# Attention with 32x32 block transposes on VectorE and P x V in 32-row, 64-column TensorE tiles

## What is computed

```python
q = rmsnorm(x @ wq_a.T) @ wq_b.T            # 32 heads, 64 plain + 64 rotary columns
kv = rmsnorm(ckv) @ wkv_b.T                 # ckv: 64 latent columns for all heads
scores = einsum("bqhd,bkhd->bhqk", q_full, k_full) * scale
scores = where(causal, scores, min)
attn = softmax(scores, axis=-1)
out = einsum("bhqk,bkhd->bqhd", attn, v)    # B=2, S=1024, H=32
out = out.reshape(B, S, H * VD) @ wo.T
```

## Time and profile before

| | |
|---|---|
| median of three runs | 2180.91 us (2177.37 to 2185.91) |
| the profiled execution: its own time | 2179.61 us |
| the profiled execution: span of the trace | 2177.8 us |
| TensorE matmuls busy, share of the span | 94% |
| VectorE, ScalarE, GpSimd busy | 52%, 44%, 52% |

### The profile page before, as it was taken

One profiled execution on the slowest core, in us unless ns is written; L12 is line 12 of the kernel. 1 busy time (PEld: TensorE's weight loads), 2 busy tenths in 40 slices (PEclk: granted clock), 3 DMA queues, 4 the chain that ended last, 5 costly groups with the idle time before them and its releaser, 6 DMA issues. The chain is left out here.

```text
span 2177.8 us, 36515 instructions
## 1 busy us (share of the span) xinstructions
PE 2045.7 (94%) x11088; PEld 1617.7 (74%) x11088; DVE 1131.3 (52%) x2607; ACT 965.1 (44%) x2162; POOL 1122.5 (52%) x834
## 2 busy tenths in 40 slices
PE   1899798999999999999999999999969999996999
PEld 1688688777777777777777777777748888875787
DVE  6655276566656666666666566666642111114453
ACT  3221075566666666666666666666641101003110
POOL 2331110888888888888888888888600000004321
PEclk9999999999999999999999999999989999998999
DMA  5652242111121122112111211221174232304421
GB/s 147 210 174 105 86 131 90 46 41 56 59 64 36 53 65 65 39 54 65 39 55 59 64 36 53 65 65 34 38 230 130 81 112 82 110 35 177 145 88 67
DMA packets 96888, 182.59 MB, mean 84 GB/s; under 512 B 16576, under 2 KB 53568, under 8 KB 94528
## 3 DMA queue, kind: packets, MB, share of 16 engines
q1 hardware_dynamic: 96832, 181.87, 26.5%
HBM read 122.85 MB, written 58.98 MB: 83 GB/s over the span
## 5 line engine op out<-in xcount | busy, mean ns | idle before, releaser
L951 PE MATMUL psS<-keyT,q 128*128 128x256 f32 (+2 forms) x2304 | 514.0, 358 | 4.3 <-POOL q L1168 4.3
L951 PEld LDWEIGHTS psS<-keyT,q 128*128 128x128 f32 x2304 | 382.9, 189 | 87.0 <-DVE negmax L1098 26.3
L1037 ACT ACTIVATE prob<-prob,negmax 128x128 f32<-128x128 f32 (+7 forms) x512 | 393.2, 771 | 74.7 <-DVE negmax L1098 74.7
L1098 DVE CUSTOM_DVE_ANT_0 prob<-psS,mask 128x128 f32<-128x128 f32 (+7 forms) x512 | 381.7, 755 | 80.4 <-PE psS L951 55.3
L1044 ACT ACTIVATE pT<-psT 128x512 f32<-128x512 f32 (+2 forms) x384 | 202.1, 526 | 350.1 <-PE psT L962 348.4
L1129 DVE COPY pT<-psT 128x256 f32<-128x256 f32 (+3 forms) x384 | 196.9, 513 | 305.1 <-PE psT L962 302.2
L962 PE MATMUL psT<-ident,prob 128*128 128x128 f32 x2304 | 338.1, 274 | 1.7 <-ACT prob L1037 1.1
L482 PE MATMUL f_psy<-f_weff,f_xT 128*128 128x512 f32 x1344 | 311.4, 391 | 0.0
L1326 PE MATMUL o_psy<-o_w,o_o 128*128 128x512 f32 x1344 | 304.8, 389 | 0.0
L962 PEld LDWEIGHTS psT<-ident,prob 128*128 128x128 f32 x2304 | 268.6, 140 | 33.0 <-issue 11.4
L1326 PEld LDWEIGHTS o_psy<-o_w,o_o 128*128 128x128 f32 x1344 | 252.3, 188 | 52.4
(11 more groups left out here) (108 smaller groups left out, 2017.5 us busy)
## 6 DMA issues: line engine op xcount, KB each, us to landing
wo<-in_wo SPq DMA_DIRECT2D x16, 1024.0 KB, 5.3
o_scale<-row_scales SPq DMA_DIRECT2D x64, 256.0 KB, 3.4
oT<-o_sum SPq DMA_DIRECT2D x128, 128.0 KB, 2.3
o_in<-oT SPq DMA_DIRECT2D x32, 512.0 KB, 5.2
f_xt<-in_x SPq DMA_DIRECT2D x16, 512.0 KB, 4.1
f_w_in<-in_w SPq DMA_DIRECT2D x16, 512.0 KB, 6.3
w_sum<-f_w_in SPq DMA_DIRECT2D x16, 512.0 KB, 5.1
x<-f_xo SPq DMA_DIRECT2D x16, 512.0 KB, 2.6
```

The lines of the kernel that those rows point to most:

```text
L951: ins = nc.tensor.matmul(psS[:, li % 2, shift + x0:shift + x1], q[:, s % 2, a, t * P:(t + 1) * P], k.keyT[:, m, b * S + x0:b * S + x1], st ...
L1037: nc.scalar.activation(row, row, ACT.Exp, bias=negmax[:, li % 8:li % 8 + 1], scale=-1.0, accum_out=rowsum[:, col:col + 1]).then_inc(exped, 1)
L1098: nc.vector.tensor_tensor_reduce(out=prob[:, li % 4, 0:(t + 1) * P], in0=place(s, t), in1=k.mask[:, S - (t + 1) * P:S], scale=-1.0, scalar ...
```

## The change

A step is now a pair of heads in one batch: 32 steps of 16 tiles (`n`; tile `t = n // 2`, head `e = n % 2`). T moves from TensorE to VectorE, which turns each 32x32 block in place. So row group `i` (partitions 32i to 32i+31) of `pT` holds 32 keys of a block and the queries of the i-th quarter of a tile. P x V therefore runs in eight tiles of 32 rows and 64 columns: four row groups, each with a PSUM bank of its own, and two halves of the output for the two heads. The values are loaded once, after the latents phase has stored them, with each 32-key block in each of the four row groups (`val`, 32 DMAs).

```diff
-    for kt in range(blocks):                                   # T on TensorE
-        ins = nc.tensor.transpose(psT[...], prob[:, (QT * s + t) % 4, ...], k.ident[:])
+    nc.vector.transpose(pT[t // 4][:, n % 2, t % 4, 0:width],  # T on VectorE
+                        prob[:, n % RING, 0:width]).then_inc(turned, 1)
```

```diff
-    for half, kts in enumerate(columns):                       # V
-        ins = nc.tensor.matmul(psV[half * KVR:(half + 1) * KVR, n0:CHUNK], k.val[:, b * QT + kt, :],
-                               pT[ch][:, kt, n0:CHUNK], ...)
+    for kt in kts:
+        t0 = max(kt - 4 * ch, 0)
+        for a in range(BLOCKS):
+            for e in range(2):
+                for i in range(BLOCKS):
+                    rows, x = slice(32 * i, 32 * i + 32), kt * P + 32 * a
+                    ins = nc.tensor.matmul(psV[KVR * e:KVR * e + KVR, i, 32 * t0:P].rearrange(...),
+                                           val[rows, b, a, kt, :], pT[ch][rows, e, t0:QT // 2, x:x + 32], ...)
```

```diff
-    nc.scalar.activation(qf[:, ch, :], psM[:, :], ACT.Copy)    # Q: one copy, and four GpSimd operations
+    nc.scalar.activation(qf[:, n % 2, :], psV[:, n, :], ACT.Copy)
+    nc.scalar.activation(swapped[64:96, n % 2, :], psV[96:128, n, :], ACT.Copy)
+    nc.scalar.activation(swapped[96:128, n % 2, :], psV[64:96, n, :], ACT.Copy)   # and three on GpSimd (A)
-    nc.vector.tensor_copy(q[..., HI, ...], qf[...])            # high part of q
+    nc.scalar.activation(q[..., HI, ...], qf[...], ACT.Copy)   # H; the low part (B) stays on GpSimd
```

```diff
-    # join on VectorE, then scale on GpSimd
+    for i in range(BLOCKS):                                    # O on VectorE: scale out of PSUM
+        ins = nc.vector.tensor_tensor(by_block(o_sum[:, ch, :], i), psV[:, i, 0:P].rearrange(...),
+                                      by_block(o_scale[:, ch, :], i), ALU.mult)
```

```diff
+PARTS = ((0, (0, 1, 2, 3)), (1, (0, 1)), (1, (2, 3)), (1, (4, 5, 6, 7)))       # V0: queries 0-511; V1 to V3: 512-1023
+PE_STEP = ("F1+0 Q0+1 S12+0 S13+0 Q1+1 S14+0 W0+0 S15+0 Q2+1 Q3+1 S0+1 S1+1 S2+1 S3+1 S4+1 S5+1 S6+1 S7+1 V1+0 V2+0 "
+           "V3+0 S8+1 S9+1 V0+1 S10+1 F0+1 S11+1")
+POOL_STEP = ("A1-1 B0-1 B1-1 A2-1 A3-1 B2-1 B3-1 A0+0")
```

More of the change, by code:

```diff
@@ L939, in scores, with queries @@
-            def scores(it, s, t):
-                li, b = QT * s + t, (s // 2) % 2
-                if later(it * TILES + li - 1, 1):
-                    pe.wait_ge(maxed, it * TILES + li - 1)
+                ins.then_inc(f_done, 1)
+            def queries(it, n, s):
+                ch, e, b = n // 2, n % 2, s % 2
+                pe.wait_ge(f_split, folds(it, e, s - s % 2 - 1))
+                for i, (a, m) in enumerate(PASSES):
+                    for t in range(QRT):
+                        ins = nc.tensor.matmul(psV[:, n, :], wq[:, a, e, t, :], k.qnT[:, m, t, b * S + ch * CHUNK:b * S + (ch + 1) * CHUNK],
+                                               start=(i == 0 and t == 0), stop=(i == 2 and t == QRT - 1))
+                ins.then_inc(q_done, 1)
@@ new lines, in query_hi, with exponentials @@
+            def query_hi(it, n, s):
+                act.wait_ge(roped, (it * 2 + s) * 4 + n + 1)
+                nc.scalar.activation(q[:, n % 2, HI, n // 2 * CHUNK:(n // 2 + 1) * CHUNK], qf[:, n % 2, :], ACT.Copy).then_inc(q_hi, 1)
+            def exponentials(it, n, s):
+                step, width = it * 2 + s, (n // 2 + 1) * P
+                act.wait_ge(maxed, step * TILES + n + 1)
+                if n % 8 == 0 and later(step, 2):
+                    act.wait_ge(recip, step * 2 - 3 + n // 8)
+                row = prob[:, n % RING, 0:width]
+                nc.scalar.activation(row, row, ACT.Exp, bias=negmax[:, n % 8:n % 8 + 1], scale=-1.0,
+                                     accum_out=rowsum[:, column(n, s):column(n, s) + 1]).then_inc(exped, 1)
@@ L1125, in copy_turned @@
[L1125 to L1130 removed]
+                    dve.wait_ge(valued, (step - 1) * NV + (1 if t < 4 else NV))
+                nc.vector.transpose(pT[t // 4][:, n % 2, t % 4, 0:width], prob[:, n % RING, 0:width]).then_inc(turned, 1)
@@ L1180, in body @@
+            pool.wait_ge(tab_in, 48)
             def body(r):
-                jobs = list(r.jobs(POOL_STEP))
-                job, n, s = list(STEADY.jobs(POOL_STEP))[-1]
-                before = None if r.first else (job, n, s - 4)
-                for job, n, s in jobs:
+                job, n, s = list(Round(0).jobs(POOL_STEP))[-1]
+                before = None if r.first else (job, n, s - 2)
+                for job, n, s in r.jobs(POOL_STEP):
                     if before:
-                        pool.wait_ge(q_lo if before[0] == "Q" else o_scaled, r.it * 8 + 2 * before[2] + before[1] + 1)
+                        pool.wait_ge(roped if before[0] == "A" else q_lo, (r.it * 2 + before[2]) * 4 + before[1] + 1)
```

506 lines of the change are left out of this document (235 added, 271 removed).

## The result

The changed kernel takes 2589.1 us (median of 4, 2577.0 to 2605.9) against 2181.9 us before: a ratio of 1.187 (95% interval 1.180 to 1.194). It is slower by 407 us. The forecast was 2100 us and the range ended at 2265 us, so both the sign and the range were missed.

What follows compares the result with a forecast made beforehand. TensorE's list was taken to set the pace at 37.4 us a step; the path's terms summed to 34.5, gaining 93 us over 32 steps and losing 14 at the ends: 2179.6 - 93 + 14 = 2100 us, range 2020 to 2265.

Steps and rivals of the forecast that it cites:

- (1): TensorE's P x V jobs V1 to V3: 5.9 us, plus 0.5 for drain and handover, 6.4 us a step.
- (2): VectorE's O operations for queries 512 to 1023, four that overlap a little: 0.9 us.
- (3): SyncE's O store, then scales stored, read back and landed, while VectorE waits for `o_scale`: 7.3 us.
- (4): Second O 0.9, the query matmuls in its bank 1.7, three copies 1.8: 4.4 us.
- (5): GpSimd's eight operations on the queries, with ScalarE's high parts fitting between: 11.0 us.
- (6): Zigzag of scores and maxima from tile 1 to tile 7, with a VectorE transpose and R: 4.5 us.
- V0's 2.4 us: TensorE's first P x V job, four blocks of each width: 2.4 us, ending 3.5 us before the scales land.
- second rival: VectorE's transposes cost twice the copies' slope, 9.1 us more: step about 38.0 us, 2212 us; chance 0.10.
- The clock: TensorE's granted clock was read as 1.00 (2.4 GHz) in the attention phase of the kernel before.
- The first rival: Row tiles in P x V don't pass one another: V1 to V3 11.8 us, step 40.4 us, 2290 us; chance 0.15.
- its break-even of 16 ns a pass: Step breaks even at 37.0 us, V1 to V3 at 8.4 us: 16 ns pass to pass, against 11.5 counted.
- The third rival: Almost no gain: each wait a little longer, or TensorE's 768 loads a step at 14 to 17 ns: 2150 to 2200 us; 0.10.

Runs made afterwards that it cites:

- v_looped: Changed kernel with P x V issued from short inner loops repeating key tiles, 832 passes a step, TensorE's loop body 1511 instructions instead of 3541: 2269 us.
- v_quarter: Changed kernel with P x V done only for the first 32 keys of every 128, three quarters of that product left out: 2210 us.
- pe_unrolled: Changed kernel with TensorE's list written out for all 16 pairs in place of a loop, nothing left out: 2502 us.
- v_looped_wide: As v_looped, but each P x V pass moves both heads' columns and every second key block is left out, so about half the passes: 2229 us.
- v_half: Changed kernel with P x V done only for the first 64 keys of every 128, TensorE's loop body 2005 instructions: 2296 us.

## Why the prediction was wrong, point by point

The terms of the prediction's path, beside one step of the changed kernel (1001.65 to 1052.86, the rows above) and one of v_looped (1004.48 to 1044.66), in us:

| term | forecast | changed kernel | v_looped |
|---|---|---|---|
| (1) V1 to V3 with handover | 6.4 | 15.0 | 9.0 |
| (2) first O | 0.9 | 0.9 | 0.9 |
| (3) until the second O begins | 7.3 | 8.4 (behind V0) | 6.8 (behind `o_scale`) |
| (4) second O, Q, copies | 4.4 | 9.8 | 7.1 |
| (5) GpSimd's eight operations | 11.0 | 11.0 | 10.9 |
| (6) zigzag to V1 | 4.5 | 6.1 | 5.5 |
| sum | 34.5 | 51.2 | 40.2 |

- **The step that failed** is "If all eight tiles run side by side, it takes two pass lengths ... 5.9 us", term (1), and with it V0's 2.4 us. It counted what the array does, and put at nothing what it takes to bring 1536 instructions a step to it. Measured: 14.8 us from V1's start, and 5.8 us for V0. Pages fetched too slowly are by far the larger part. The array's part was nearly right: at the full clock a quarter of V1 to V3 took 1.91 us (v_quarter), and less the 0.22 us of its last pass, four such quarters are 6.8 us (an estimate). The miss of 0.9 us there is mostly in the narrow passes, put at 0.11 us for 16, 6.9 ns each; pe_unrolled's last piece of V3 has them at 10.4 ns ((1.26 - 0.22) / 100). The other 8 us of the 14.8 are stalls for pages, and the lower clock behind them.
- Of the 15.7 us between the forecast's step and the measured one, the loop adds 3.6 us (50.2 to 46.6), the rest of the fetching some 7.1 us (46.6 to 39.5), and 0.8 us (39.5 to 38.7) go with fewer passes and hidden turns. By the medians these three are 2.7, 7.3 and 1.2 us a step; the changed kernel's profiled execution was the slowest of its four. As v_looped has more passes and its inner loops' turns, the share of the fetching is probably put too low.
- What is left, 38.7 against 34.5 us, are mostly terms (4) and (6). The first queries' matmuls stand on TensorE behind scores, and in every second step behind the folds too. In v_looped, from 600 to 1400 us, (4) averages 7.1 us in the steps with folds and 4.7 in the others, where I counted 4.4 (the step shown has folds; the next, without, took 38.0 us). I read the path in the right order, but in (4) left out the folds, which stand ahead of Q in the list. The fetching and the order of SyncE were undone by runs, one at a time; (4) and (6) are read from timelines and not tested.
- **The clock.** The forecast took 1.00 throughout. The stretch shows 0.85, with the passes behind stalls at the lower level (2.92 us for six against 1.56). It came back to 0.99 when the stalls went (v_looped), so it is a consequence of TensorE's idle time and not its cause; but not of the fetching alone, since it stayed at 0.85 in v_quarter, where TensorE waited for other engines. How many of the 7.1 us are its share, no run separates.
- **VectorE** was right: 1.241 us for 1024 columns (1.25 forecast), O at 0.284, and it is never the bound. The second rival falls: 1024 columns take 1.24 us, not 2.3. GpSimd, the lengths of SyncE's operations and the order of the path were right.
- **The first rival** had the sign and not the mechanism: row tiles do pass one another (v_looped_wide). Straight code stays below its break-even of 16 ns a pass: 14.3 ns at 128 columns and less at fewer.
- **The third rival** named the loads and their instructions, "at 14 to 17 ns", with 2150 to 2200 us. v_looped's average is 16.5 ns with its turns, and it took 2269 us, with (4) and (6) longer than forecast as well.
- I took the strict order of matmuls in the Trainium skill ("TensorE: Matmul & The Clock Gate", Part 3, The mechanism) to mean that a matmul's second pass holds up the next tile's first. v_looped_wide contradicts that reading, with 288 passes in 6.83 us, and the same section says itself that matmuls in different tiles overlap, with which the trace agrees. The floor of about 25 ns between starts (Part 1) does not hold here from tile to tile, where a pass comes every 14.3 ns; as an estimate for V a step (19 us, measured 20.6) it was nearer than mine, for another reason.

## What to carry to other kernels

Before cutting matmuls into small tiles, count the instructions of TensorE's loop body and how long a page of 256 lasts: a body of 2005 or more was fetched again in each pass, a page took 3.5 us to come, and a page of 32-row, 128-column passes is used up in about 2 us, one of large matmuls in some 20 us. Then count the passes: eight tiles side by side brought a pass of 128 columns every 14.3 ns, about what its columns need, but one of 64 or 32 columns only every 10.4 ns, so narrow passes gain little; and an inner loop that keeps the body short costs some 0.2 us a turn. When one long engine becomes short, the waits behind it are the next bound; here the order of two items on SyncE was worth 2.8 to 2.9 us of some 38 a step, but only once P x V was out of the way.

## What the runs showed of the hardware

- The instruction queue's packets stand in the page's DMA part. One page for TensorE is 16.4 KB, 256 instructions, and comes every 3.47 us when it is waited for (pe_unrolled).
- A loop body of 1511 instructions was not fetched again (v_looped), one of 2005 was (v_half). A loop that doesn't fit costs more than its pages: about one page a step more than is executed (4.9 against 3.9 in v_half; 8.0 against 6.9 in the changed kernel), and a stall of 2 to 3 us at its top.
- In 32x64 tiles, eight of them side by side, a load and a pass of 128 float32 columns come every 14.3 ns in straight code, and of 64 or 32 columns every 10.4 ns (both pe_unrolled). 208 of them, most with 256 columns, come in 5.28 us, about 25 ns each, and there the columns set it (v_looped_wide).
- A turn of an inner loop on TensorE, 64 passes of 128 columns with its instructions at hand, takes some 0.2 us more than its passes (1.14 us, v_looped).
- VectorE's 32x32 transposes run at 1.04 ns a column: (1241 - 306) / 896.
